# Layer normalisation of finished query tiles: sum on GpSimd, centring on ScalarE, moments and root in half steps of their own

## What is computed

```python
def _layernorm(x, g, b):
    m = jnp.mean(x, axis=-1, keepdims=True)
    v = jnp.mean((x - m) ** 2, axis=-1, keepdims=True)
    return (x - m) / jnp.sqrt(v + EPS) * g + b
z = _mha(x, x, Wq1, Wk1, Wv1, mask0, causal=True)          # L0: no output projection
x1 = _layernorm(x + z, ln1_g, ln1_b)
...
sa = _mha(x, x, x, tgt_mask, sa_wq, ..., sa_wo, sa_bo)     # L2: with wo and bo
x = _ln(x + sa, ln1_g, ln1_b)
```

## Time and profile before

| | |
|---|---|
| median of 3 runs | 2725.34 us (2723.77 to 2726.54) |
| the profiled execution's own time | 2719.28 us |
| its span, first to last instruction | 2717.3 us |
| mean granted TensorE clock | 0.956 |
| busy share TensorE / VectorE / ScalarE / GpSimd | 92 / 66 / 51 / 27% |

### The profile page before, as it was taken

The page is one execution under the profiler, slowest core; times in us unless marked ns, Lnnn a source line. Parts: engine busy times, 40 slices in busy tenths (PEclk is TensorE's granted clock), DMA queues, the critical chain, the costliest instruction groups (busy, mean ns, idle before and its releaser), DMA issues. The chain is left out here.

```text
span 2717.3 us, 44289 instructions
## 1 busy us (share of the span) xinstructions
PE 2500.1 (92%) x16014; PEld 1373.0 (51%) x16014; DVE 1783.6 (66%) x4364; ACT 1381.5 (51%) x1921; POOL 739.8 (27%) x867
## 2 busy tenths in 40 slices
PE   6999999988999999997999997799999999797896
PEld 3544433333444444443999997334434444385553
DVE  3566777777677777774457774577777777455554
ACT  1544455544555555555357875255555555452332
POOL 2243335433321110201016564102222112223012
PEclk7999999989999999998899999699999999998998
DMA  6222222122133223220127785422322322001331
GB/s 177 53 50 71 58 61 65 37 54 61 43 96 94 70 75 92 78 53 25 40 86 217 221 221 130 115 71 78 108 61 73 91 73 60 9 1 42 83 85 41
DMA packets 102212, 218.54 MB, mean 80 GB/s; under 512 B 19116, under 2 KB 35372, under 8 KB 100716
## 3 DMA queue, kind: packets, MB, share of 16 engines
q1 hardware_dynamic: 93164, 203.66, 27.5%
q0 software_dynamic: 8832, 12.06, 2.4%
HBM read 100.34 MB, written 12.58 MB: 42 GB/s over the span
## 5 line engine op out<-in xcount | busy, mean ns | idle before, releaser
L1120 ACT ACTIVATE probT_a<-scores 128x1024 f32<-128x1024 f32 (+3 forms) x832 | 779.0, 947 | 712.5 <-PE scores L951 420.6
L1228 DVE CUSTOM_DVE_ANT_0 ring<-ring,maskb_a 128x512 f32<-128x512 f32 x1024 | 686.3, 716 | 172.9 <-PE ring L969 163.6
L969 PE MATMUL ring<-stacks_a 64*128 64x512 f32 (+7 forms) x1664 | 468.2, 461 | 53.3 <-DVE negm_a L1226 17.3
L990 PE MATMUL outputs<-probT_a,V_a 128*32 128x512 f32 (+6 forms) x3328 | 443.9, 576 | 12.5 <-ACT oT_a L1129 8.5
L1226 DVE TENSOR_REDUCE negm_a<-ring 128x1 f32<-128x512 f32 (+3 forms) x640 | 332.1, 563 | 139.7 <-PE ring L975 105.4
L930 PE MATMUL scores<-stacks_a 64*128 64x512 f32 (+7 forms) x1664 | 399.7, 449 | 2.4 <-DMA stacks_a<-narrow_a 2.4
L969 PEld LDWEIGHTS ring<-stacks_a 64*128 64x128 f32 (+1 forms) x1664 | 211.7, 190 | 376.0 <-issue 140.2
L930 PEld LDWEIGHTS scores<-stacks_a 64*128 64x128 f32 (+1 forms) x1664 | 170.7, 187 | 249.6 <-issue 151.9
L889 POOL TENSOR_SCALAR maskb_a<-ints_a 128x1024 bf16<-128x1024 int32 x31 | 112.8, 3639 | 423.5 <-DMA ints_a<-in_mask 353.4
L899 POOL TENSOR_TENSOR ve<-mv,epsilon 128x1 f32<-128x1 f32 x96 | 18.2, 190 | 725.0 <-DVE mv L1195 725.0
L951 PE MATMUL scores<-maskT_a,identb 64*64 64x512 bf16 x1024 | 211.0, 402 | 0.0
(11 more groups left out here) (240 smaller groups left out, 3741.0 us busy)
## 6 DMA issues: line engine op xcount, KB each, us to landing
stacks_a<-parts_a SPq DMA_DIRECT2D x672, 128.0 KB
raw<-in_moew SPq DMA_DIRECT2D x92, 512.0 KB, 3.9
ints_a<-in_mask SPq DMA_DIRECT2D x31, 512.0 KB, 3.7
swapped_a<-maskT_a SPq DMA_DIRECT2D x32, 256.0 KB, 3.7
wt<-in_w SPq DMA_DIRECT2D x7, 1024.0 KB, 4.9
kvT_a<-in_ctxT SPq DMA_DIRECT2D x12, 512.0 KB, 3.4
wrow<-in_row SPq DMA_DIRECT2D x7, 512.0 KB, 5.9
stacks_a<-narrow_a SPq DMA_DIRECT2D x224, 8.0 KB
```

The lines of the kernel that those rows point to most:

```text
L969: last = pe.matmul(bank("S", j, n, e)[:, 0:w], Q[rows, g, qt * P:(qt + 1) * P], K[rows, g, 0:w], start=True, stop=not a.causal)
L990: last = pe.matmul(OB[x * slot:(x + 1) * slot, q0:S], V[:, m % 2, kb, c:c + slot], probT[:, kb % 2, x, q0:S], start=(kb == 0), stop=(kb == ...
L1120: act.activation(probT[:, kb % 2, 2 * p:2 * p + 2, q0:S], scores_bank(j, n)[:, :, q0:S], ACT.Exp, bias=0.0, scale=-1.0).then_inc(c_exp.sem, 1)
L1228: least = dve.tensor_tensor_reduce(sc, sc, maskb[:, m % 2, qt, :], 1.0, BIG * 2, ALU.add, ALU.min, out)
```

## The change

A stage is "aside" if it ends in a layernorm and has 16 columns a head: stages 1, 2, 5 and 6. For their units, but not for the last unit of a block:

- Tiles finish every second half step instead of every one (`on` at 3, 5, 7, 9).
- The sum with the tokens is a new entry `res` on GpSimd, in the half step of `on` (or of `y`, where VectorE keeps the bias sum).
- The moments are an entry `mom` one half step later, on VectorE, waiting for that sum; `root` in the same half step on GpSimd: variance plus epsilon, power, and a new third instruction, shift = -mean x root.
- The centring is an entry `cen` one half step later on ScalarE: root x y + shift as one activation. GpSimd's gain (`ln`) stands in the same half step.

L0's feed-forward keeps its sums on VectorE; its root moves into the half step of `fy`, its centring goes to ScalarE two half steps later with the gain behind it (20, 22, 24, 26). `fx` moves from 9 and 10 to 12 and 13, `fh` from 13 and 15 to 14 and 16, `tokens` from 16 to 17, `norms` from 20 to 21. Stages 3, 4 and 7 keep their work and its order.

```diff
+        self.aside = ln and dk == 16
...
     for qt in range(QT):
-        t = qt + late
-        out += [(2 + t, "on", -1, qt), (3 + t, "ot", -1, qt), (4 + t, "y", -1, qt),
-                (t + (5 if a.wo else 3), "ln", -1, qt)]
+        t = qt * (2 if a.aside else 1) + late
+        summed = t + (4 if a.wo else 2)
+        out += [(2 + t, "on", -1, qt), (3 + t, "ot", -1, qt), (4 + t, "y", -1, qt)]
+        out += [(summed, "res", -1, qt), (summed + 1, "mom", -1, qt), (summed + 1, "root", -1, qt)]
+        out += [(summed + (2 if a.aside else 1), "cen", -1, qt), (summed + (2 if a.aside else 1), "ln", -1, qt)]
...
+    out += [(12, "fx", -1, 0), (13, "fx", -1, 1), (14, "fh", -1, 0), (16, "fh", -1, 1)]
+    for qt in range(QT):
+        out += [(18 + 2 * qt, "fy", -1, qt), (18 + 2 * qt, "froot", -1, qt), (20 + 2 * qt, "fcen", -1, qt),
+                (20 + 2 * qt, "fl", -1, qt)]
...
+        def aside(j):
+            return att[units[j][0]].aside and j + 1 < base + len(units)
...
+                if kind == "res" and aside(j):
+                    st, b, a, k = stage_of(j)
+                    pool.wait_ge(*c_rD.at("y" if a.wo else "on", j, n))
+                    pool.wait_ge(*two_before(c_centred, j, n))
+                    pool.tensor_tensor(y[:, n % 2, :], plain[n % 2][:, :] if a.wo else o[:, n % 2, :], tile(b, n), ALU.add)\
+                        .then_inc(c_summed.sem, 1)
+                if kind in ("root", "froot"):
...
+                    pool.wait_ge(*c_mean.at(*key))
+                    pool.tensor_tensor(ve[:, r, :], mv[:, r, 1:2], eps_of[a.eps], ALU.add)
+                    pool.drain()
...
+                        pool.tensor_tensor(rstd[:, r, :], ve[:, r, :], minus_half[:, 0:1], ALU.pow)
+                        pool.drain()
+                        pool.tensor_scalar(shift[:, r, :], mv[:, r, 0:1], rstd[:, r, :], -1.0, ALU.mult, ALU.mult)\
+                            .then_inc(c_root.sem, 1)
...
+                if kind == "fcen" or (kind == "cen" and aside(j)):
+                    r = n % 2
+                    key = (j, n) if kind == "cen" else ("f0", j, n)
+                    act.wait_ge(*c_root.at(*key))
+                    act.wait_ge(*two_before(c_done, *key))
+                    act.activation(xh[:, r, :], y[:, r, :], ACT.Identity, bias=shift[:, r, :], scale=rstd[:, r, :])\
+                        .then_inc(c_centred.sem, 1)
...
+                if kind == "mom" and aside(j):
+                    dve.wait_ge(*c_summed.at(j, n))
+                    moments_of(n)
```

More of the change, by code:

```diff
@@ L156, in timetable @@
     out += [(2 * h + 2 + n * step, "mT", 1, n) for n in range(QT)]
-    out += [(2 * h, "cnld", 2, 0), (2 * h, "tokens", 2, 0), (2 * h + 2 * step, "norms", 2, 0),
+    out += [(2 * h, "cnld", 2, 0), (2 * h + step // 2, "tokens", 2, 0),
+            (2 * h + 5 * step // 2, "norms", 2, 0),
             (2 * h + 3 * step, "kvld", 2, 0), (3 * h, "x", 2, 0), (3 * h, "x", 2, 1)]
@@ L282, in build @@
     rstd = sb("rstd", [P, 2, 1], F32)
+    shift = sb("shift", [P, 2, 1], F32)
     ss = sb("ss", [P, QT], F32)
@@ L328, in build @@
     c_count = sem("c_count")
+    c_summed = tally("c_summed")
     c_mean = tally("c_mean")
@@ L1244, in _ @@
                     dve.tensor_reduce(lens[:, n, 3:4], energy[:, n, :], AX.X, ALU.add).then_inc(c_count, 1)
-                if kind not in ("tokens", "norms", "x", "c", "q", "k", "V", "on", "y", "ln", "fx", "fy", "fl"):
+                if kind not in ("tokens", "norms", "x", "c", "q", "k", "V", "on", "y", "mom", "cen", "fx", "fy"):
                     continue
@@ L1299, in _ @@
                         dve.wait_ge(*c_ring.at("ot", j, n - 2))
+                    elif aside(j):
+                        dve.wait_ge(*c_summed.at(j, n - 2))
                     given = o[:, n % 2, :].rearrange("p (h s) -> p h s", s=a.dk)
@@ L1307, in _ @@
                         dve.tensor_tensor(given, view[:, :, 0:a.dk], share, ALU.mult).then_inc(c_rD.sem, 1)
-                    if not a.wo:
+                    if not a.wo and not aside(j):
                         dve.drain()
@@ L1317, in _ @@
                     else:
-                        dve.tensor_tensor(junk[:, :], out, wrow[:, k, 1, :], ALU.add).then_inc(c_rD.sem, 1)
-                        dve.drain()
-                        dve.tensor_tensor(y[:, n % 2, :], junk[:, :], tile(b, n), ALU.add)
-                        moments_of(n)
+                        if aside(j):
+                            dve.wait_ge(*c_summed.at(j, n - 2))
+                        dve.tensor_tensor(plain[n % 2][:, :], out, wrow[:, k, 1, :], ALU.add).then_inc(c_rD.sem, 1)
+                        if not aside(j):
+                            dve.drain()
+                            dve.wait_ge(*two_before(c_centred, j, n))
+                            dve.tensor_tensor(y[:, n % 2, :], plain[n % 2][:, :], tile(b, n), ALU.add)
+                            moments_of(n)
                 if kind == "fx" and n == 1:
@@ L1335, in _ @@
                     moments_of(n)
-                if kind in ("ln", "fl"):
+                if kind == "cen" and not aside(j):
                     r = n % 2
-                    key = (j,) if kind == "ln" else ("f0", j)
-                    dve.wait_ge(*c_root.at(*key, n))
-                    dve.wait_ge(*c_done.at(*key, n - 2))
+                    dve.wait_ge(*c_root.at(j, n))
+                    dve.wait_ge(*two_before(c_done, j, n))
                     dve.tensor_scalar(xh[:, r, :], y[:, r, :], mv[:, r, 0:1], rstd[:, r, :], ALU.subtract,
```

29 lines of the change are left out of this document (18 added, 11 removed).

## The result

The changed kernel takes **2775.9 us** (median of 4 runs, 2769.9 to 2776.5) against 2725.9 for the kernel before (4 runs): a ratio of **1.0183**, with a 95% interval from 1.0163 to 1.0203. That is 50 us slower; the forecast was 30 us slower. The profiled execution has a span of 2773.8 us, 56.5 more than the 2717.3 of before, and it is that difference which the traces can split up.

A forecast was written before the change was run, and what follows sets the result against it. TensorE, busy 92% of the span, was taken as the bound. Terms 43.9 + 10.2 - 10 - 3 - 5.6 - 3 - 2 = +30.5 us; against the median 2755.8, say 2755.5 us; range 2718 to 2786.

The forecast's parts named there:

- The stall: Six units, stages 1 to 3, steps 3 to 12: TensorE stands behind GpSimd's lengths; 146.75 becomes 190.7 us, +43.9 (0 to 58).
- The walk: Queue-order estimate for stage 1's third unit: transposes start at 226.6 instead of 220.10, step 12 comes 31.5 us after step 3.
- Rival A: Six units of the stall: TensorE has enough queued to cover it, only gains remain, -23.6, 2702 us; chance 0.13.
- nobody waits for the end of the lengths: GpSimd's 9.6 us of lengths between units: their end is wanted only a whole unit later; said to decide the forecast.
- The clock: Behind the stall in six units: 3.4 us of TensorE work at the lower level loses 1.7 each, +10.2 in all.
- Norms "counted at nothing": Tokens and norms move one step behind other GpSimd and VectorE work; what they feed is due at step 24: no cost.
- The feed-forward's end: Steps 18 to 26 of four units: root queued ahead of the norms, centring on ScalarE; -10, at least -4.
- The -3 for the 16 centrings: Feed-forward's end: 16 centrings of 0.41 us leave VectorE, 6.5 us, counted at -3 (0 to -6.5).
- Stages 5 and 6: Seven units: the walk ends 0.8 us earlier in each, -5.6 (+7 to -9); mask conversion counted apart at -3.
- rival C: Stages 5 and 6: rounds hold VectorE 1 us for each of three sums, +21 there; +57, 2782 us; chance 0.12.
- The mask term: Stages 5 and 6: first mask conversion starts some 4 us earlier on GpSimd, shortening waits for the second: -3 (0 to -4.2).
- The two units without lengths: Last unit of stage 2 and first of stage 3: the walk without the stall gives -2, bounded by 0 and -6.

The follow-up runs named there:

- experiment 1: Changed kernel with the first half's lengths moved from step 7 to step 11, behind the gain of tile 3: 2781.1 us, ratio 1.0202 to the kernel before.
- experiment 2: Changed kernel without the count of masked keys (6 of the lengths' 9.6 us) in every unit but the first: 2736.5 us, ratio 1.0045 to the kernel before.
- experiment 3: Changed kernel with the first half's lengths at step 8, behind the root of tile 2 and ahead of its gain: 2778.3 us, ratio 1.0202.
- experiment 4: Changed kernel with the norms back at step 20, tokens left where the change put them: 2766.2 us, ratio 1.0137 to the kernel before.
- experiment 8: Changed kernel with GpSimd sums only in stages 5 and 6, one tile a half step in the last unit, norms at step 20, early mask conversions: 2703.5 us.
- experiment 9: As experiment 8, but all query tiles finished on VectorE, one a half step, no sum on GpSimd: 2705.0 us, ratio 0.9922 to the kernel before.
- experiment 6: Changed kernel with query tiles finished as before the change; the feed-forward's part and later tokens and norms stay: 2722.1 us, ratio 0.9979.
- experiment 7: Changed kernel with one tile a half step, lengths at step 8 behind the gain of tile 3, and the edits of experiments 4 and 5: 2710.8 us, ratio 0.9955.
- experiment 5: Changed kernel with the mask conversions of stages 5 and 6 at steps 0 and 11, their loads earlier: 2764.8 us, ratio 1.0139 to the kernel before.

## Why the prediction was right, and where its sum was wrong

The direction, the mechanism and the place were right, and 2775.9 us lies in the range. The forecast was 20 us short. Its two largest terms came out 8 us too high together, and what made the kernel slower than forecast lies in the other terms; that these errors partly cancelled is luck.

*The stall: +43.9 forecast, +36.6 measured* (the 45.9 of the six stretches without the 9.3 of the next point). All marks named but one are in the trace: the lengths between sum and root of tile 2, ScalarE's wait of 11.13 us, stretches of 31.6 to 32.7 us, a lower granted clock behind the wait, and VectorE's wait of 2.81 us gone. The one is TensorE's wait of 6 to 8 us: it was 4.71 to 6.35 us in the six units. In the unit shown its query projection, just ahead of the wait, took 3.78 us, where the same four products take 1.94 at 233.25 in experiment 1, and so filled part of it. The walk nearly holds in time: it put the end of the sum of tile 2 14.4 us behind step 3 (213.65), the transposes 27.4 (226.6); the trace has 13.9 and 26.8. From there to step 12 the walk had 4.1 us, and the earlier trace rows with the first row of the parts above give 3.29 at the upper level. So it was 1.4 us too long in this unit; which steps make up the rest of the 7.3 is open, as the walk was written out for this unit alone. Experiments 1 to 3 show the cause. Rival A fell: what TensorE had queued did not cover the wait. The argument that decided, that nobody waits for the end of the lengths, was too wide, as experiment 1 showed; in the kernel before it held only because the order behind them left room.

*The clock: +10.2 forecast, +9.3 measured.* The forecast had 3.4 us of work at the lower level behind each stand, which loses 1.7. The trace has 4.5 to 5.6 us at a granted clock of 0.50 to 0.57 there, 1.6 us longer in the mean than before the change; with fewer matmuls in it in stage 2 (20 after, 22 or 26 before), so the clock itself may cost a little more. By step 12 it is over: from there to step 16 the granted clock is 1.00 and the stretch takes 8.05 us. What ran slowly ahead of the wait cost nothing: the projection of 3.78 us ended at 227.14, and ScalarE's copy of it, held behind the centring, began at 232.92; in all six units 5.6 to 6.5 us lie between the two.

*Norms "counted at nothing": about +5.3 in stages 3 and 4.* This is the step that failed outright. I asked when the norms' product is due (step 24) and not where VectorE's reduction of the squares, 1.21 us, would then stand. Experiment 4 takes it back. It also ate into the next term: steps 20 to 25 fell further with the norms back (experiment 4).

*The feed-forward's end: -10 forecast, -6.4 measured*, and -10.6 with the norms at their old place (experiment 8). The root ahead of the norms does what was said. The -3 for the 16 centrings does not show: the unit without norms takes 14.90 us for these steps and not 14.26. Nor did the sum say where the moved hidden layer comes to stand: its second half is now at step 16, and steps 16 to 18 of the four units take 26.08 us and not 20.46, time that was in part spent in earlier steps before.

*Stages 5 and 6: -5.6 (seven units) and -3 forecast; -2.4 and +8.7 measured* in six. The rounds did not hold VectorE up, so rival C fell: the stretches are 28.8 us, not above 30. The mask term has the wrong sign. I followed the second mask to its load on SyncE and saw that come earlier, which it does; but the conversion behind it stands in GpSimd's queue after two rounds that the first conversion has put off by 3.66 us. With the conversions out of the way the six units come to -7.0. That this is near the forecast's -8.6 is luck: -4.7 of it comes without any moved sum (465.28 to 460.54 us in experiment 9), by the earlier conversions, which the change does not have.

*The last unit of stage 6: not in the sum, +4.1.* It keeps VectorE for its tiles but took over the spacing of two half steps, with nothing to fill the gaps. I infer this from the kernels with a spacing of one, 220.5 to 222.6 us (experiments 6 to 9), against 226.5 to 229.7 for those with two; the spacing was not changed by itself.

*The two units without lengths: -2 forecast, -5.7 measured* over whole units. Their stretches from step 3 to 12 alone give -6.5; steps 20 to 25, which the feed-forward's term has already, another -3.55, and the moved feed-forward work takes most of the rest back. The number is loose: experiments 1 to 5, which leave these units' query tiles as they are, have 174.3 to 180.5 us for them, against 174.4 after the change and 180.1 before it.

*Costs counted small.* The centring on ScalarE took 598 ns, where I took 480; the shift 267 ns, where I took 200:

```profile
L1177 ACT ACTIVATE xh<-y,shift,rstd 128x256 f32<-128x256 f32 x76 | 45.4, 598 | 129.2 <-POOL shift L928 129.0
...
L928 POOL TENSOR_SCALAR shift<-mv,rstd 128x1 f32<-128x1 f32 x76 | 20.3, 267 | 13.0 <-issue 13.0
```

The estimate of 0.585 us from the Trainium skill (ScalarE: Activation LUTs, What ACT_TABLE_LOAD costs) agrees with the 598 ns. The gain's addition, which took 0.88 us beside VectorE's sum, takes 0.73 in the rounds here, where that sum has left VectorE. By the rule of the Trainium skill (SBUF - State Buffer, Who interferes with whom) it should, and the trace agrees.

What stays open: why the first unit of stage 2 ran its stretch at a granted clock of 1.00 in the kernel before, and at 0.78 to 0.87, some 3 us longer, in experiments 1, 2 and 6 to 9; how the gain in the four units with the feed-forward divides between the root, the centring on ScalarE and the later transposes, and why the norms' place is worth 4 us there in experiment 8 but nothing over the whole units in experiment 4.

## What to carry to other kernels

When work moves to an engine that has time to spare, walk that engine's queue in order, and do not go by its busy share. A hand-over between three engines makes each tile a round with waits in it, and a long instruction between two halves of a round (9.6 us of lengths, 3.66 us of mask conversion) puts off everything queued behind it. In stages 1 and 2 TensorE came to wait for that, in stages 5 and 6 only a later conversion did harm. Moving the lengths alone changed who waited, at three places; two tiles in flight, with the lengths behind the last of them, ended the stall. And for an entry that is moved, ask of every instruction in it, on every engine, what it now stands in front of, not only when its result is due.

## What the runs showed that I had not expected

A lower TensorE clock can be free in one place and cost its full price a few us later. In the stall shown, a projection took 3.78 us instead of 1.94 ahead of the wait, and nothing was lost, as ScalarE's copy of it was held for another 5.8 us anyhow. Behind the wait nothing covered TensorE, and the same 29 matmuls took 5.62 us instead of 3.29. So a granted clock averaged over a stretch (0.68 here) does not tell the loss: cut the stretch where the wait ends. And an instruction of 0.28 us on GpSimd (the selected query, behind the lengths) held TensorE for 7.03 us while the profile's releaser said only "issue": where that word stands behind a long gap, the row that ended just before it, on another engine, is the one to look for.
